# Three loads and identity products at the start of a Mamba and mixture-of-experts block

## What is computed

```
xn = layernorm(x); g = xn @ gate_w + gate_b; gate, gate_gate = silu(g halves)
u = xn * gate @ state_w + state_b; Bm = gate_gate @ state_w + state_b
delta = softplus(mean(xn @ state_w + state_b)); h = exp(-delta) * h + delta * Bm * u
x = x + y @ out_w + out_b; x = x + gelu(layernorm(x) @ mlp_w1 + mlp_b1) @ mlp_w2 + mlp_b2
```

```
moe_out = sum over the token's 2 experts of w * (gelu(xn @ ew1 + eb1) @ ew2 + eb2)
for i in range(3): moe_out = moe_out @ expm(gens[i])
gate = sigmoid(concat(abel_out, moe_out) @ gc_w + gc_b)
out = layernorm(x + residual + abel_out * (1 - gate) + moe_out * gate)
```

## Time and profile before

| | us |
|---|---|
| runs, median of 3 | 729.74 |
| runs, lowest and highest | 727.7 and 888.66 |
| the profiled execution | 730.6 |
| its span, first to last instruction | 728.7 |
| TensorE busy in the span | 632.1 |
| VectorE busy | 587.5 |
| ScalarE busy | 462.9 |
| GpSimd busy | 248.2 |

### The profile page before, as it was taken

One profiled execution on the slowest core, in us unless ns is written; L12 is line 12 of the kernel. 1 busy time (PEld: TensorE's weight loads), 2 busy tenths in 40 slices (PEclk: granted clock), 3 DMA queues, 4 the chain that ended last, 5 costly groups with the idle time before them and its releaser, 6 DMA issues. The chain is left out here.

```text
span 728.7 us, 16183 instructions
## 1 busy us (share of the span) xinstructions
PE 632.1 (87%) x4525; PEld 473.6 (65%) x4526; DVE 587.5 (81%) x1535; ACT 462.9 (64%) x876; POOL 248.2 (34%) x295
## 2 busy tenths in 40 slices
PE   6899999999999999999979995889999999996000
PEld 5667557575665857566556884678888888885000
DVE  4989768899998999899798875577788878784693
ACT  4346573956658494765757344667777777774197
POOL 2111020125436081633516540133434344444042
PEclk9999999999999999999998997999999999999555
DMA  5643223165644537356725824465666655310974
GB/s 146 197 148 58 87 42 80 55 127 193 117 152 103 135 109 157 119 103 236 171 87 176 275 99 109 112 162 148 160 166 160 164 132 126 77 58 4 303 246 144
DMA packets 124502, 99.21 MB, mean 136 GB/s; under 512 B 60432, under 2 KB 114587, under 8 KB 124316
## 3 DMA queue, kind: packets, MB, share of 16 engines
q1 hardware_dynamic: 108028, 68.82, 33.4%
q0 software_dynamic: 16416, 29.67, 17.4%
HBM read 62.42 MB, written 33.68 MB: 132 GB/s over the span
## 5 line engine op out<-in xcount | busy, mean ns | idle before, releaser
L1920 POOL DMA_INDIRECT scratch_ys<-ye,place x78 | 86.9, 1114 | 149.4 <-ACT ye L1964 109.5
L79 PE MATMUL up<-shared,words 128*128 128x256 bf16 x936 | 112.3, 278 | 13.0 <-PEq L1738 7.8
L79 PE MATMUL bank<-words 128*128 128x512 bf16 (+1 forms) x576 | 109.4, 343 | 3.8 <-DVE logits L1077 3.2
L79 PE MATMUL down<-words,shared 128*128 x936 | 110.5, 274 | 1.8 <-DVE yb L2051 1.1
L79 PEld LDWEIGHTS up<-shared,words 128*128 x936 | 93.1, 100 | 26.9 <-issue 14.3
L79 PEld LDWEIGHTS down<-words,shared 128*128 128x128 bf16 x936 | 90.8, 98 | 15.9 <-issue 3.6
L79 PE MATMUL bank<-xn_s,mlp_w 128*128 128x512 bf16 x384 | 89.5, 387 | 2.2 <-DVE xn_s L798 2.2
L79 PEld LDWEIGHTS bank<-words 128*128 128x128 bf16 x576 | 55.4, 98 | 50.4 <-issue 6.6
L79 PE MATMUL bank<-mlp_w,shared 128*128 128x256 bf16 x768 | 86.4, 273 | 0.0
L510 POOL DMA_INDIRECT scratch_zs<-rows,pos x64 | 71.0, 1109 | 37.2 <-DVE pos L1127 18.5
L79 PEld LDWEIGHTS bank<-mlp_w,shared 128*128 128x128 bf16 x768 | 74.9, 98 | 10.6 <-issue 0.4
(11 more groups left out here) (247 smaller groups left out, 1151.4 us busy)
## 6 DMA issues: line engine op xcount, KB each, us to landing
fetched<-scratch_zs SPq DMA_DIRECT2D x156, 64.0 KB
words<-scratch_ys SPq DMA_DIRECT2D x16, 514.0 KB, 8.5
scratch_abel<-staged SPq DMA_DIRECT2D x8, 514.0 KB, 3.7
abel_all<-scratch_abel SPq DMA_DIRECT2D x8, 514.0 KB
x_in<-in_x SPq DMA_DIRECT2D x8, 512.0 KB, 5.6
words<-in_out_b_row SPq DMA_DIRECT2D x8, 512.0 KB, 4.1
fetched<-in_mlp_b_row SPq DMA_DIRECT2D x8, 512.0 KB, 3.5
words<-in_x POOLq DMA_DIRECT2D x8, 512.0 KB, 7.9
```

The costliest lines, as they stand in the source:

```text
L79: last = nc.tensor.matmul(dst, lhs(a, k), rhs(b, k), start=start and n == 0, stop=stop and n == total - 1)
L1920: nc.gpsimd.indirect_dma_start(out=ys_dram[:, :], out_offset=bass.IndirectOffsetOnAxis(ap=place[:, k, s:s + 1], axis=0), in_=ye[:, k % 2, ...
```

## The change

The load of the generators becomes three transfers, one for each generator, each with a semaphore of its own. TensorE waits for each generator alone before its transposes; VectorE waits for all three, as before. A new helper, busy(n), issues n products of the identity with itself into the first 128 columns of bank 3, whose contents nobody reads before the next product of bank 3 writes over them. These are plain products, not transposes. It is called with 10 ahead of the first transposes, behind the wait for the identity, and with 14 behind the transposes of the first tokens.

```diff
-        gens_in, thr_r, norm_r, all_norm, sq_r, mat_r, turned, aT_r, prod_done = [sem(n) for n in (
-            "gens_in", "thr_r", "norm_r", "all_norm", "sq_r", "mat_r", "turned", "aT_r", "prod_done")]
+        gens_in = [sem(f"gens_in{k}") for k in range(GENS)]
+        thr_r, norm_r, all_norm, sq_r, mat_r, turned, aT_r, prod_done = [sem(n) for n in (
+            "thr_r", "norm_r", "all_norm", "sq_r", "mat_r", "turned", "aT_r", "prod_done")]
...
-            sp.dma_start(A, t["gens"].rearrange("g (k p) n -> p g k n", p=P)).then_inc(gens_in, 16)
+            for s in range(GENS):
+                sp.dma_start(A[:, s], t["gens"][s].rearrange("(k p) n -> p k n", p=P)).then_inc(gens_in[s], 16)
             load_x(0, 0)
...
-            dve.wait_ge(gens_in, 16)
+            for s in range(GENS):
+                dve.wait_ge(gens_in[s], 16)
             absolute_rows(A, 0)
...
+            def busy(n):
+
+                for _ in range(n):
+                    nc.tensor.matmul(bank[3][:, 0:P], ident[:, :], ident[:, :], start=True, stop=True)
+
             def round_turns(n, lhs):
                 for s in range(GENS):
                     if isinstance(n, int) and n == 0:
-                        pe.wait_ge(gens_in, 16)
+                        pe.wait_ge(gens_in[s], 16)
...
+            busy(10)
             round_turns(0, A)
             round_products(0, A)
             round_turns(GENS, A2)
             turn1(0)
+            busy(14)
             round_products(GENS, U, True)
```

## The result

The changed kernel takes 725.0 us in the median of 18 runs; the kernel before, in 18 runs of its own, 728.04. The ratio is 0.9961, with a 95% interval from 0.9949 to 0.9974: 2.8 us, between 1.9 and 3.7. One of the eighteen runs of before took 888.66 us; it is an outlier, and the ratio leaves it out. The profiled execution of the changed kernel has a span of 723.1 us, 5.6 under that of before.

What follows compares the result with a forecast made beforehand. TensorE was taken as the bound, with VectorE also on the opening's path. Load -0.0, VectorE -1.7 and a wait -0.5 gave -2.2 (728.4 from 730.6); with the median 0.9 lower and 2.1 taken, 727.6 us; range 725.2 to 731.0.

Steps and rivals of the forecast that it cites:

- the sum: Whole kernel: load -0.0, VectorE -1.7, the wait at 48.09 -0.5, together -2.2 us; 728.4 from 730.6.
- Ten identity products: Before the first transposes: two instructions each, 0.43 us at the low clock; ten take 4.3 us, ending at 6.15.
- Landing: Generator load: if three transfers run like one, seen near 4.5, 5.15 and 5.8 us; the split gives TensorE nothing.
- the first rival: Generator load: three transfers in series each pay a start, last generator and tokens late; far end 734.9 us; chance 0.06.
- the prediction's own signs of being wrong: Opening: first transposes after 7 us, statistics after 8.6, products at 0.427 until 11, or second round at half pace.
- Clock: TensorE's first round: clock rises at 6.9 us, products end at 13.0 instead of 14.9; 13.9 if it rises at 8.7.
- VectorE: Opening: token statistics, rows and copies end at 14.1 us instead of 15.8, a gain of 1.7.
- Fourteen identity products: Before TensorE's second round: they take 3.0 us, the stall is 1.4 us instead of 4.2, the clock very likely stays.
- Where the two meet: After the first squaring: VectorE's updates move by 1.7 us, the transposes at 49.18 by 2.2; 1.5 with the clock low.
- the gain is given back later: A later wait, at the hand-over to the experts, takes the gain back: 729.7 us; chance 0.16.
- the clock isn't raised sooner: First round: identity products don't count, clock rises at 10.96 us as before, products end at 15.0; 729.8 us; chance 0.10.
- all goes well: Opening: clock up at 5.3 us, tokens on time, VectorE gains 2.1, ScalarE's chain up to 3.2; 726.5 us; chance 0.08.

Runs made afterwards that it cites:

- the one of three loads with the root on ScalarE: Changed kernel with the first tokens' inverse root on ScalarE (logarithm, exponential) instead of GpSimd: 723.27 us, ratio to the kernel before 0.9931.
- second pair of profiles: The kernel before and the changed kernel each run once more, unchanged: 730.55 and 725.12 us.

## Why the prediction was right, and where not

The forecast was 2.1 us less, by an opening that only shifts what is behind it; measured are 2.8 (1.9 to 3.7). The predicted time, 727.6 us, lies above the measured 725.0 mostly because the median of before was 729.74 in three runs and 728.04 in eighteen; for the same reason 725.0 lies just under the lower end of the range, 725.2, which as a difference reached to 4.5 us less. That the total came out near the forecast is in part luck: at the transposes the opening gave 1.7 us in the first pair of profiles and 1.1 in the second, less than the 2.2 of the sum, and stretches behind 370 us, which the sum left out, gave about 1 more.

*Ten identity products* were put at two instructions each, 4.3 us, ending at 6.15: measured 5.92. That they take the whole lead of the early generators, so that the split gives TensorE nothing, held in both executions of the changed kernel; in the one of three loads with the root on ScalarE the third generator came behind them and TensorE waited for it till 7.46.

*Landing* was wrong in its condition "if three transfers run like one". They don't. VectorE's first reduction, which needs them all, began between 6.4 and 7.5 us in the seven profiles with three loads, and at 5.75 to 6.1 in the six with one. The windows of the DMA queue (length, clock, DMA share, GB/s) of the kernel before and of the changed one:

```profile
3.75:5.25 1.50, 1.00 1.09 382
```

```profile
3.75:5.25 1.50, 1.00 0.72 144
```

With one load 378 to 384 GB/s moved in that stretch, with three 144 to 206, in all thirteen profiles. Why the rate drops there was not tried, so whether each piece pays a start of its own is open. In effect it is a small form of the first rival, about 0.9 us and not 7.3, too little to decide; it did reach one of the prediction's own signs of being wrong, the statistics after 8.6, in the second execution (8.82; 8.52 in the first). The fixed 2 us for each transfer, which the prediction took from the Trainium skill, DMA: Bandwidth & Descriptors, stands there for transfers that GpSimd issues. These are issued by SyncE, and two more of them cost 0.3 to 1.8 us together, not 4.

*Clock*: forecast to rise at 6.9, bounds 5.3 and 8.7; it rose at 5.5 and 7.4 in the two executions of the changed kernel. The end of the products was forecast at 13.0: 12.5 and 13.4.

*VectorE* is the step that failed in size. It was to gain 1.7 us at the start of the right-hand sides. Up to the last copy it gained 1.45, but the step took everything from there to the right-hand sides as a chain that moves with VectorE. It doesn't: GpSimd's reduction can't begin before 5.5 us after its own power, and the power came later, ending at 11.74 where it had ended at 10.89, since the generators were seen late. So 0.64 us were left, and 0.13 in the second pair of profiles. In the trace of before the 5.5 us were covered by a wait of 7.02 us for the norm, which looked like idle time.

*Fourteen identity products*: 3.0 us forecast, 3.1 measured; the stall 1.4 and 1.9; the clock stayed, as forecast, in the six profiles where a stall of 1.1 to 2.2 us was left behind them, and fell in all five without them. This term was not priced by itself in the sum, which counted it only as a difference between 2.2 and 1.5. The experiment without the fourteen shows that, with three loads, it is the whole effect: there the second round began 0.20 us before that of the kernel before (21.40, 21.60) and ended 0.04 before it (28.46, 28.50), with the clock low from its first instruction to 24.7 us, and the transposes came 0.03 us earlier. The 1.5 us forecast for a low clock were too many, since they leaned on VectorE's 1.7, of which 0.20 existed in that run (right-hand sides at 20.50).

*Where the two meet*: 2.2 us forecast, 1.7 and 1.3 measured from the first profile of before, since VectorE's term was smaller by 1.1 and its third update had 0.49 us and more to take up.

*The rivals.* That the gain is given back later is refuted up to 370 us by the table, and behind it by the totals. That the clock isn't raised sooner is refuted (5.5 and 7.4 against 10.96). That all goes well was beaten by the measured total, but by stretches behind 370 us and not by the opening it named. The measured 2.8 us less the 1.7 us by which the two profiles of each differ at the stall behind 370 leave 1.1 us. The clocks of the runs put a size on it. The time at 0.50 in a run is 2 x (1 - granted clock) x span: 71.6 us on average in the eighteen runs of the changed kernel, 77.7 in the sixty runs of before beside the experiments. Of the 6.1 less, 3.4 are the fall in the opening, and half of the other 2.7, about 1.3 us, is an estimate of what they cost behind it. So the 1.1 us are not the chance of one profile. The prediction took a gain in the total without one at 50 us, or the reverse, as the refutation of an opening that only shifts the rest. Neither came in full, but the two part by 1 to 3 us in every kernel with the fourteen: up to 370 us the opening shifts the rest and no more, and behind it something else is at work, whose cause is open.

## What to carry to other kernels

Price an engine's silent time before you count it as idle: a wait of 7 us ended by another engine can hide 5.5 us of its own work, which comes out when the other gets faster. Work without use that keeps TensorE's clock up pays only where the real work behind it is on the path, so test each filler alone: here, with three loads, the one ahead of the first load was worth nothing that the total shows, the one ahead of the second round everything. Splitting a load let its first part arrive 2 us sooner here and its last part 0.3 to 1.8 us later; who waits for all of it pays. And when two versions come out alike, look at what held each of them up before you call a delay harmless.

## What the runs showed of the hardware

GpSimd changes from elementwise operations or constants to the reduction over partitions at a price of 5.5 to 7.1 us, and back to add and power at 7.3 to 7.5. The profile shows two MODIFY_POOL_CONFIG records where the change begins and nothing in the engine's row while it lasts. It is made during the next operation's wait, not after it: with the change early and the wait long (reduction at 16.49 behind a norm at 16.36) nothing of it shows. A float32 product of 128 columns takes two instructions, 0.216 us at the high clock, a transpose of the same shape one, 0.109 us. With three loads of 256 KB the queues moved 144 to 206 GB/s in the stretch from 3.75 to 5.25 us, with one of 768 KB 378 to 384, and the last of the three was seen 0.3 to 1.8 us later than the one. Work of 326 us behind an opening of 47 to 56 us keeps its length within 0.5 us.
